# A transformer kernel on one core: GpSimd's scatters and gathers without their waits for TensorE, and another order of the loads, stores and weights on the loading queue

## The reference

```python
x = x + _L0_attn_ref(_layernorm(x), ...)   # 2 sequences of 512, 16 heads, a triangular solve
x = x + _L0_ffn_ref(_layernorm(x), ...)    # 64 experts, 8 for each token, capacity 256 rows
x = x + _L1_attn_ref(_layernorm(x), ...)   # linear attention, a running sum over the tokens
x = x + _L1_ffn_ref(_layernorm(x), ...)    # 8 experts, 2 for each token

# the part that the change is about, _L0_ffn_ref
scores, idx = jax.lax.top_k(softmax(x @ gate_w.T), 8)
xbuf = zeros((64, 256, 256)).at[e_sorted, pos].set(x[tok_sorted], mode='drop')
g = einsum("ecd,efd->ecf", xbuf, w_gate)   # 256 -> 96
u = einsum("ecd,efd->ecf", xbuf, w_up)
y = einsum("ecf,edf->ecd", silu(g) * u, w_down)
out = zeros((1024, 256)).at[tok_sorted].add(y[e_sorted, safe_pos] * (s_sorted * valid)[:, None])
```

## Time and profile before

| | |
|---|---|
| median of the runs | 1025.71 us |
| the profiled execution | 1016.34 us, its span 1014.6 us |
| granted TensorE clock, mean | 0.837 |
| PE busy | 708.1 us (70%) |
| PEld busy (weight loads) | 566.9 us (56%) |
| DVE busy | 549.2 us (54%) |
| ACT busy | 313.5 us (31%) |
| POOL busy | 252.2 us (25%) |
| DMA | 151.73 MB, mean 150 GB/s |

### The profile page before, as it was taken

The page is one execution under the profiler, slowest core; times in us unless marked ns, Lnnn a source line. Parts: engine busy times, 40 slices in busy tenths (PEclk is TensorE's granted clock), DMA queues, the critical chain, the costliest instruction groups (busy, mean ns, idle before and its releaser), DMA issues. The chain is left out here.

```text
span 1014.6 us, 17699 instructions
## 1 busy us (share of the span) xinstructions
PE 708.1 (70%) x6542; PEld 566.9 (56%) x6587; DVE 549.2 (54%) x1652; ACT 313.5 (31%) x535; POOL 252.2 (25%) x258
## 2 busy tenths in 40 slices
PE   4858377858757786973156999999205763599995
PEld 2423265446436545842145999999204542599994
DVE  6896986799499679263501333333146675022221
ACT  1004143542444355432022444444003451111110
POOL 6003011120211111016762000000575626023222
PEclk9988779979887898597577999999756675699998
DMA  4981002340631358204947888887422204688760
GB/s 136 137 130 48 0 2 46 156 63 3 199 51 14 125 211 319 96 17 146 320 142 251 288 290 291 294 283 248 130 76 68 81 26 156 244 229 249 221 195 1
DMA packets 75561, 151.73 MB, mean 150 GB/s; under 512 B 12768, under 2 KB 36064, under 8 KB 72544
## 3 DMA queue, kind: packets, MB, share of 16 engines
q1 hardware_dynamic: 62064, 124.27, 39.7%
q0 software_dynamic: 10224, 21.12, 7.4%
q10 hardware_dynamic: 3200, 5.38, 1.6%
HBM read 91.01 MB, written 60.43 MB: 149 GB/s over the span
## 5 line engine op out<-in xcount | busy, mean ns | idle before, releaser
L1375 PE MATMUL scores<-wgu,zero 128*128 128x192 f32 x512 | 98.2, 337 | 3.7 <-DMA wd<-in_wd 3.7
L750 DVE TENSOR_REDUCE block_maxima<-scores 128x10 f32<-128x1280 f32 x64 | 92.3, 1486 | 7.7 <-PE scores L400 6.7
L1032 ACT ACTIVATE E<-scores 128x1280 f32<-128x1280 f32 x64 | 77.3, 1238 | 60.6 <-PE scores L411 32.4
L1476 DVE TENSOR_TENSOR gated_up<-gated,scores 128x192 f32<-128x192 f32 x64 | 22.7, 354 | 123.7 <-ACT gated L1517 123.7
L1375 PEld LDWEIGHTS scores<-wgu,zero 128*128 128x128 f32 x512 | 85.6, 197 | 3.9 <-DMA wd<-in_wd 3.9
L1815 PE MATMUL scores<-xgT,w 128*128 128x128 f32 x736 | 87.8, 278 | 0.0
L1815 PEld LDWEIGHTS scores<-xgT,w 128*128 128x128 f32 x736 | 86.0, 196 | 0.1
L1170 POOL TENSOR_SCALAR_AFFINE_SELECT E<-E 128x256 f32<-128x256 f32 x64 | 27.2, 449 | 205.8 <-ACT E L1032 205.7
L1508 ACT COPY zero<-misc 128x512 f32<-128x512 f32 x64 | 37.5, 586 | 98.3 <-PE misc L1368 98.3
L1392 PE MATMUL scores<-wd,gated_turned 96*128 96x256 f32 x256 | 67.0, 385 | 0.5 <-ACT gated_turned L1504 0.5
L2116 POOL DMA_INDIRECT gb<-expert_outputs,gather_slots x48 | 55.0, 1147 | 33.7 <-DVE X L1939 17.0
(11 more groups left out here) (295 smaller groups left out, 1500.4 us busy)
## 6 DMA issues: line engine op xcount, KB each, us to landing
w<-in_w SPq DMA_DIRECT2D x23, 1024.0 KB, 5.0
expert_rows<-zero SPq DMA_DIRECT2D x32, 512.0 KB, 6.2
xg<-expert_rows SPq DMA_DIRECT2D x64, 256.0 KB, 3.2
expert_outputs<-xnT SPq DMA_DIRECT2D x64, 256.0 KB, 3.0
wgu<-in_wgu SPq DMA_DIRECT2D x32, 384.0 KB, 3.6
rows_by_expert<-zero SPq DMA_DIRECT2D x21, 408.0 KB, 6.0
wd<-in_wd SPq DMA_DIRECT2D x32, 192.0 KB, 3.8
w<-in_w ACTq DMA_DIRECT2D x8, 512.0 KB, 10.3
```

The costliest lines, as they stand in the source:

```text
L750: nc.vector.tensor_reduce(bm[:, c, h, :], scores[:, slot, 0:WIDE].rearrange("p (a n) -> p a n", n=P), AX.X, ALU.max).then_inc(s_fd, 1)
L1032: nc.scalar.activation(to[:, h, :], scores[:, k % 2, 0:WIDE], ACT.Exp, scale=SCALE).then_inc(s_fa, 1)
L1375: ins = nc.tensor.matmul(scores[:, j % 2, t * 2 * F0:(t + 1) * 2 * F0], xgT[:, j % 2, k, t * P:(t + 1) * P], wgu[:, j // GE, j % GE, k, :] ...
```

## The change

Four edits. All the waits of GpSimd for counters of TensorE go. `EARLY` falls from 16 to 10, so six scatters of the first half move from block one to block two. TensorE's first turn of an expert's rows waits for the slots (`s_idx`) rather than for the routing weights (`s_w8`). On the loading queue, block two begins with four groups of weights rather than three, then come the rows of experts 0 to 7 with the stores of experts 0 to 3 between and behind them, then the rows of experts 8 to 13 with weight groups 4 and 5 and the stores of experts 4 and 5; from expert 8 on the loop is as before.

```diff
-EARLY = 16
+EARLY = 10
@@ block one, GpSimd
                     for g in range(EARLY):
-                        if g == 4:
-                            pool.wait_ge(s_us, 4 * UNITS)
-                        if g == 6:
-                            pool.wait_ge(s_o, 2 * UNITS - 1)
...
                         scatter(pool, g // HT, g % HT, xn0[:, g % HT, :])
@@ block two, TensorE
-                    pe.wait_ge(s_w8, 1)
+                    pe.wait_ge(s_idx, 4)
@@ block two, GpSimd
                     for g in range(EARLY, HT * K0):
-                        if g == EARLY + 4:
-                            pool.wait_ge(s_tr, 12)
...
                         scatter(pool, g // HT, g % HT, xn0[:, g % HT, :])
                     pool.wait_ge(s_idx, 4)
                     for k in range(K0):
                         for t in range(HT):
-                            if t == 0 and k > 5:
-                                pool.wait_ge(s_y0, k - 5)
-                            if t == 1 and k > 1:
-                                pool.wait_ge(s_t, k - 1)
-                            if t == 2 and k > 4:
-                                pool.wait_ge(s_th0, k - 4)
-                            if t == 3 and k > 2:
-                                pool.wait_ge(s_gu, k - 2)
                             scatter(pool, k, HT + t, xn[:, t, :])
...
-                        if g % 2:
-                            pool.wait_ge(s_gu, min(E0, E0 - 2 + g // 2))
-                        elif g:
-                            pool.wait_ge(s_y0, min(E0, E0 - 5 + g // 2))
@@ block two, the loading queue
-                    for w in range(NW - 1):
+                    for w in range(NW):
                         load_weights(w, w)
-                    for e in range(NB - GE):
+                    for e in range(NB):
+                        if e >= 5:
+                            store(e - 5, e - 5)
                         load_rows(e, e)
+                    store(NB - 5, NB - 5)
+                    for e in range(NB, 2 * NB - GE):
+                        sp.wait_ge(s_t, e - NB + 1)
+                        load_rows(e - NB, e)
+                        if e == NB + 1:
+                            sp.wait_ge(s_y0, GE)
+                            load_weights(0, NW)
+                        if e == NB + 3:
+                            store(4, 4)
+                            sp.wait_ge(s_y0, 2 * GE)
+                            load_weights(1, NW + 1)
+                        if e == NB + 4:
+                            store(5, 5)
@@ block three, GpSimd
                         pool.wait_ge(s_acc0, g - NG + 1)
-                        if r == 3 and q > 1:
-                            pool.wait_ge(s_oo, QT * (q - 1))
-                        if r == 4 and q:
-                            pool.wait_ge(s_tr, 12 + at_lin(q - 1) + 1)
...
```

More of the change, by code:

```diff
@@ L1596, in body @@
                                 store((j - 2) % NB, e - 2)
-                    steps(sp.Fori, E0 // NB, body)
+                    body(1, False, False)
+                    with sp.Fori(2, E0 // NB - 1) as i:
+                        body(i, False, False)
+                    body(E0 // NB - 1, False, True)
                     store(NB - 2, E0 - 2)
@@ L2103, in _ @@
                         t, k = gather_at(g)
-                        q, r = divmod(g - NG, GQ)
                         pool.wait_ge(s_acc0, g - NG + 1)
-                        if r == 3 and q > 1:
-                            pool.wait_ge(s_oo, QT * (q - 1))
-                        if r == 4 and q:
-                            pool.wait_ge(s_tr, 12 + at_lin(q - 1) + 1)
-                        if r == 7 and q:
-                            pool.wait_ge(s_pr, 2 * q - 1)
-                        if r == 8 and q > 1:
-                            pool.wait_ge(s_tr, 12 + at_ffn(q - 2) + 1)
-                        if r == 10 and q:
-                            pool.wait_ge(s_pr, 2 * q)
                         pool.indirect_dma_start(
```

## The result

The changed kernel took 1055.82 us (median of 4 runs, 1055.4 to 1057.19) against 1024.91 for the kernel before (4 runs): ratio 1.0301, interval 1.028 to 1.0322. It is slower by 31 us. The forecast was 1009.4, so it was wrong in sign. The profiled execution took 1055.57, its span is 1053.8 and its mean clock 0.826.

A forecast was written before the change was run, and what follows sets the result against it. Block two was taken as bound by GpSimd's scatters, then TensorE, its end by GpSimd again. Gains 11.1 + 2.0 + 3.6 less 0.4 made 16.3, off 1025.7: 1009.4 us; own range 1005.5 to 1012, with rivals 1004.5 to 1017.

The forecast's parts named there:

- the removed waits among the scatters: Blocks one and two: GpSimd's waits were nearly all met when reached; only one 4.30 us idle mattered, gain 4.0 us.
- First gathers: End of block two: the second gather no longer waits 2.24 us for TensorE, gain 2.0 us.
- Block three: Block three: gathers run ahead without holds, so windows start sooner; gain 3.6 us, bounded by 0 and 12.
- the gain does not carry: Rival, chance 0.05: runs without a profile, 9.4 us longer for an unseen reason, stay within 3 us of 1025.7.
- The rival that ended slower: Chance 0.05: on the one loading queue, rows of experts 8 to 14 take 6.2 us each, ending at 1033 us.
- The block change: Block one to two: six scatters fewer free other engines 7.7 us sooner; gain 1.4 us at the second half.
- The hole: Block two, before 512.19: a 4.30 us idle of GpSimd, its scatter waiting for TensorE's first turn; gain 4.0 us.
- the hole is not TensorE's: Rival, chance 0.09: traffic held that scatter in block two, so 4.0 us stays, giving 1013.4 us.
- Weight group 3: Block two, expert 6: loaded at the start, it ends the 3.66 us wait of gate and up; gain 3.7 us.
- no cold step: Block two: gate and up of expert 6 start warm, 1.47 us rather than 2.93; gain 2.0 us.
- A late run-in: Rival, chance 0.15: rows of expert 8 and weight group 4 come late in block two, TensorE stalls; 1015.1 us.
- VectorE holds the gathers: Rival, chance 0.11: VectorE's work blocks GpSimd's gathers in block three, losing the 3.6 us gain; 1013.0 us.

The follow-up runs named there:

- late session: Session whose runs of the kernel before had a median of 1023.9, 1025.9 or 1025.0 us; all its profiles show signals arriving long after the signalling engine finished.
- prompt condition: That of sessions whose runs of the kernel before had a median of 1014.9, 1016.7 or 1016.5 us; none of their profiles has a late signal.
- the single removal: Kernel before without GpSimd's waits among the second half's scatters in block two, nothing else changed, in a prompt session: 1010.05 us, ratio 0.9957.
- the pause kernel: Changed kernel with a small memset that GpSimd waits for before every fourth scatter and gather of block two, late session: 1038.79 us, ratio 1.0121.
- few pauses: Changed kernel with twelve pauses of GpSimd (a small memset it waits for) and block three's waits back, late session: 1031.42 us, ratio 1.0064.

## Why the prediction was wrong

The step that failed is *the removed waits among the scatters*: "nearly all met when GpSimd came to them", costed as stalls of GpSimd and nothing else. (Block one has five of these waits, not eight; its row to row time hid no cost of them.) *First gathers* and *Block three* stand on the same step. In a late session the waits were also the stops in which other engines' signals arrive. Without them the ranks came 15.4 us late, gate and up of expert 1 19.7, and block three took 11.3 us more than that of the kernel before in a late profile (293.9 against 282.6). The loss by stage, counted from the first scatter of block one and against that late profile: second half's first scatter +12.9 us, first gather +16.2, block three's start +14.8, end +26.1.

The second step that failed is the last of the sum: "I take the same difference off it". The profile was 9.4 us faster than the median of the runs for the same program. I gave this 0.05, as *the gain does not carry*, within 3 us of no change. It was the mark that profile and runs came from different conditions, the rival nearest to the truth, and much too small in size and chance. The rival that ended slower, the loading queue, didn't happen: rows and weights came in time. None of the rivals named late signals; the profile shown has none, so no row of it could have priced them.

By its own steps, in the prompt condition that its rows came from, with the times from the first scatter of block one (451.40 before, 453.62 after):

- *The block change*: 7.7 sooner for the other engines; measured 15.56 against 23.46, 7.9. At the second half 1.4; measured 1.5. Right, with GpSimd idle 2.9 us across the change of block against 3.1.
- *The hole*: last scatter 5.4 sooner; measured 536.96 - 453.62 = 83.3 against 88.9, 5.5. Right, and the single removal gained 4.8 where the hole was priced at 4.0. The rival *the hole is not TensorE's* falls.
- *Weight group 3* and *no cold step*: steady experts begin 93.9 us behind the first scatter, not 103.2: 9.3 sooner, forecast 11.1. The wait is gone, but the step was 2.45 us and not 1.47, so the 2.0 was mis-sized by about half: TensorE had been idle for 2.91 us, and the turn between was slow as well (1.12 against 0.66). The new queue alone gained 4.6, for 3.7 + 2.0. *A late run-in* falls.
- *First gathers*: block three started 11.5 sooner; forecast 12.7.
- *Block three*: 5.3 shorter (278.3 to 273.0); forecast 3.6. The two kernels without these waits but with the old queue gained more, 9.6 and 9.8 (268.7 and 268.5). The difference to 273.0 goes with TensorE's clock: between 40 and 80 us behind the first gather of block three it was granted at 0.68 and 0.67 (two stretches of 20 us) in the trace with 273.0, and at 0.76 and 0.76 in the one with 268.5, and the projections took 29.0 us in the first and 24.5 in the second. After the same work, with an idle of 5.4 and 5.7 us ahead of it, twelve of their matmuls took 4.80 us at 773.83 in the first and 2.86 at 776.12 in the second; why the clock rose later is open. The gather of 4.84 us stayed, and the others took at most 1.74. The rival *VectorE holds the gathers* falls. By the Trainium skill, SBUF — State Buffer, section "Who interferes with whom", an instruction of VectorE with two inputs in this memory, as the adds have, contends with a GpSimd instruction that reads it. The one gather of 4.84 us beside 17 adds could be such a case, but many other gathers met single adds of this kind and took about 1.02, so the forecast's "this trace agrees" was too strong, and no run shows a loss by it.
- *The early waits*, costed at nothing beyond 1 us: some 4 in the medians (998.21 against 994.21), 1.2 of it seen between the first scatter of block two and that of the second half. The profiles don't show the rest.

Together 16.8 us from block one on in the profiles, where 16.3 were forecast; the medians say 22.4. The profile was that of the slowest of six runs, 7.5 us above their median; a block three at the faster clock would make up 4.5 of this, but no trace of a faster run is kept. The time, its sign and its range were wrong where it was measured.

Open: what in the hardware holds the signals back, and what makes a session late. Shown is that the late ones lie in rows of indirect DMAs or within 5 us behind them (the late traces of the changed kernel and of the kernel before have none ahead of the first scatter), that breaks of about 1.1 us every four keep nearly all prompt, and that the same program in another session has none. That a backlog builds up over a row and drains in breaks was only argued. For it: in the late trace of the kernel before the picks keep their 0.21 us until 504.48, 7.5 us into a row, and lag from 505.50 on, as they did with few pauses. Against a plain form of it: of the 94 waits of ScalarE and VectorE that the nine late profiles put down to "remote" from 400 us on, 44 end while a row goes on, and the ranks of the pause kernel were 2.6 us late behind three scatters. Of the 12.5 us between the two profiles of the kernel before, 7.4 arise between block one's scatters and block three, beside its late signals, and 4.3 in block three, where the signal of the second routing is 4.9 us late.

## What to carry to other kernels

If a profile and the timed runs of one program differ by more than the runs among themselves, settle that first: here 9.4 us (0.9%) told of a condition in which the change had the other sign. A wait that is always met can still do work; before removing several, ask what stops the engine once they are gone, and measure in more than one session.

## What the runs showed of the hardware

- In some sessions a counter's increment reaches a waiting engine up to 19.7 us late where GpSimd issues indirect DMAs every 1.28 us; in others, with the same program, 0.1 us after the matmuls. It is not only TensorE's counters: VectorE's own came up to 2.5 us late.
- A stop of GpSimd brings many of them: 1.8 us into a wait, 1.0 us into a pause of 1.12. It isn't the only way: nearly half of them (44 of 94) come while a row goes on, as at 459.97 in the changed kernel.
- The condition holds for a whole session: 17, 8 and 15 runs of the kernel before at 1012 to 1021 us, 1, 21 and 11 at 1022 to 1029, and no session with both. Chip 0 had a session of either kind.
